# A fused graph network on one core: register loads of the one-hot loop gathered ahead of a wait, and the attribute split of the message loop spread over two steps

## What is computed

```python
x = x + L0(h, edges)          # mean of neighbours, two matrix products
x = x + L1(h, edges, noise)   # four transformer blocks with attention over edges
x = x + L2(h, edges, attr3)   # graph convolution; weight of an edge from 3 attributes
x = x + L3(h, edges, attr64)  # messages on edges
# L3:
edge_feat = concatenate([x[src], x[dst], edge_attr])   # 20000 x (512 + 512 + 64)
messages  = mish(mish(edge_feat @ W1 + b1) @ W2 + b2)
agg       = segment_sum(messages, dst)
# ... two more products on the nodes, a layernorm
```

## Time and profile before

| | us |
|---|---|
| median of 3 runs | 1679.72 |
| the runs | 1679.72, 1692.11, 1679.65 |
| profiled execution, its time | 1672.88 |
| profiled execution, its span | 1671.0 |
| busy in the span: PE / DVE / ACT / POOL | 1566.8 / 1190.2 / 1097.2 / 686.0 |

### The profile page before, as it was taken

How to read it: one execution, slowest core, us unless ns; L and a number is a source line. 1 busy time by engine, 2 the same in 40 slices (tenths; PEclk the granted TensorE clock), 3 DMA queues, 4 the chain that set the end, 5 groups by cost and what they waited for, 6 DMA issues and landing times. The chain is left out here.

```text
span 1671.0 us, 25082 instructions
## 1 busy us (share of the span) xinstructions
PE 1566.8 (94%) x8530; PEld 1218.3 (73%) x8530; DVE 1190.2 (71%) x1900; ACT 1097.2 (66%) x1531; POOL 686.0 (41%) x495
## 2 busy tenths in 40 slices
PE   5789699999999999999999999999999999999987
PEld 4765486878687868877854777777777777777774
DVE  8867546564655546565733588989989898998967
ACT  9841536554554455444530699999999999999962
POOL 3410120110012001200302788888888888888500
PEclk9999799999999999999999999999999999999989
DMA  3001140013002200211107767677777777777710
GB/s 104 0 19 65 39 133 25 1 51 113 26 20 67 85 21 32 62 52 63 53 1 228 156 139 150 145 144 148 138 152 144 148 145 142 151 135 155 162 38 31
DMA packets 107046, 153.94 MB, mean 92 GB/s; under 512 B 42042, under 2 KB 47034, under 8 KB 106466
## 3 DMA queue, kind: packets, MB, share of 16 engines
q0 software_dynamic: 72832, 87.84, 27.3%
q1 hardware_dynamic: 34146, 65.21, 12.0%
HBM read 141.02 MB, written 11.73 MB: 91 GB/s over the span
## 5 line engine op out<-in xcount | busy, mean ns | idle before, releaser
L1692 POOL DMA_INDIRECT edge_gathered<-dst_table,edge_index x158 | 257.3, 1629 | 57.4 <-issue 53.9
L222 PE MATMUL edge_z2p<-edge_w_hi,edge_h_hi 128*128 128x512 f32 x628 | 255.3, 407 | 6.8 <-issue 3.5
L1661 POOL DMA_INDIRECT edge_gathered<-src_table,edge_index x158 | 221.5, 1402 | 85.3 <-issue 33.6
L222 PE MATMUL edge_z2p<-edge_w_hi,edge_h_lo 128*128 128x512 f32 x628 | 248.5, 396 | 0.0
L222 PE MATMUL edge_z2p<-edge_w_lo,edge_h_hi 128*128 128x512 f32 x628 | 248.3, 395 | 0.0
L904 POOL TENSOR_TENSOR tr_cw<-w_c,tr_cw 32x1024 fp32r<-32x1024 f32 x8 | 19.0, 2373 | 367.5 <-ACT tr_cw L1118 367.5
L915 POOL TENSOR_TENSOR h<-h,tr_row_b 128x512 f32<-128x512 f32 x40 | 61.1, 1562 | 263.9 <-ACT C L1160 263.6
L222 PEld LDWEIGHTS edge_z2p<-edge_w_hi,edge_h_hi 128*128 128x128 f32 x628 | 117.9, 188 | 61.3 <-issue 36.3
L2020 DVE SCALAR_TENSOR_TENSOR edge_early<-edge_early,edge_z1p 128x1024 f32<-128x1024 f32 x79 | 96.5, 1221 | 59.8 <-ACT edge_early L1897 44.0
L222 PEld LDWEIGHTS edge_z2p<-edge_w_hi,edge_h_lo 128*128 128x128 f32 x628 | 118.0, 188 | 28.5
L222 PEld LDWEIGHTS edge_z2p<-edge_w_lo,edge_h_hi 128*128 128x128 f32 x628 | 118.1, 188 | 24.9
(11 more groups left out here) (356 smaller groups left out, 3985.8 us busy)
## 6 DMA issues: line engine op xcount, KB each, us to landing
w_c<-in_attr_T SPq DMA_DIRECT2D x78, 128.0 KB
agg<-edge_sum_rows POOLq DMA_DIRECT2D x36, 128.0 KB
w_a<-in_wv SPq DMA_DIRECT2D x4, 1024.0 KB, 5.3
w_b<-in_wq SPq DMA_DIRECT2D x4, 1024.0 KB, 5.4
w_a<-in_wk SPq DMA_DIRECT2D x4, 1024.0 KB, 7.7
w_b<-in_wo SPq DMA_DIRECT2D x4, 1024.0 KB, 7.0
w_a<-in_m SPq DMA_DIRECT2D x4, 1024.0 KB, 5.4
w_b<-in_m SPq DMA_DIRECT2D x4, 1024.0 KB, 5.3
```

The source lines that it names most:

```text
L222: mm = pe.matmul(out, a, b, start=(n == 0), stop=(n == last))
L1661: pool.indirect_dma_start(out=from_rows[a][:, j, :].bitcast(F32), out_offset=None, in_=k.src_table, in_offset=bass.IndirectOffsetOnAxis(ap ...
L1692: pool.indirect_dma_start(out=from_rows[ring][:, j, :].bitcast(F32), out_offset=None, in_=k.dst_table, in_offset=bass.IndirectOffsetOnAxis ...
```

## The change

In `front`, the loads of window starts: one for the two groups of a span in place of one for each group, in the prologue and in the loop. In the loop the start of the addition and the start of the two later compares are both loaded ahead of the wait on group_ready. In the two spans behind the loop the load also stands ahead of the wait.

In `edge_layer`, on DVE: the copy of the attribute split (L2040) moves from the end of the even step to the end of the odd step before it, for the group of the coming step; the subtraction stays. Its wait on z1_made asks for s(-1), in the odd step, where it was s(-2) in the even one. In step 0, which has no step before it, both stay together. The hand-written last steps follow the same conditions.

```diff
-                for a in range(RING):
-                    compare_to(a, a, start_of(a))
+                for a in range(0, RING, SHARE):
+                    start = start_of(a)
+                    for b in range(SHARE):
+                        compare_to(a + b, a + b, start)
...
-                def add_span(u, s, a):
-                    start = start_of(u)
+                def add_span(s, a, start):
                     dve.wait_ge(added, s + 2)
...
                         u = t * RING + a
+                        start, start_next = start_of(u), start_of(u + RING)
                         dve.wait_ge(group_ready, u + (SHARE + RING))
                         for b in range(SHARE):
-                            compare_to(u + (RING + b), a + b, start_of(u + (RING + b)))
-                        add_span(u, t * (RING // SHARE) + a // SHARE, a)
+                            compare_to(u + (RING + b), a + b, start_next)
+                        add_span(t * (RING // SHARE) + a // SHARE, a, start)
                         for b in range(SHARE):
                             compare_from(u + (RING + b), a + b)
                 for a in range(0, RING, SHARE):
+                    start = start_of(n * GROUPS + (GROUPS - RING + a))
                     dve.wait_ge(group_ready, n * GROUPS + (GROUPS + a + SHARE))
...
+                def attr_high(slot, group):
+                    dve.wait_ge(attr_loaded[slot], group // 2 * 32 + 32)
+                    dve.tensor_copy(attr_parts[slot][:, :], attr[slot][:, :]).then_inc(S["attr_high"], 1)
...
                     if a % 2 == 0 and on(0):
                         slot = a // 2
-                        dve.wait_ge(attr_loaded[slot], g(0) // 2 * 32 + 32)
-                        if on(4):
-                            dve.wait_ge(S["z1_made"], s(-2))
-                        dve.tensor_copy(attr_parts[slot][:, :], attr[slot][:, :]).then_inc(S["attr_high"], 1)
+                        if not on(1):
+                            attr_high(slot, g(0))
                         dve.wait_ge(S["attr_high"], g(-2))
                         dve.tensor_tensor(attr_parts[slot][high, :], ...).then_inc(S["attr_low"], 1)
+                    if a % 2 == 1 and on(-1):
+                        if on(3):
+                            dve.wait_ge(S["z1_made"], s(-1))
+                        attr_high((a + 1) % 4 // 2, g(-1))
```

More of the change, by code:

```diff
@@ L625, in _ @@
                 for a in range(0, RING, SHARE):
+                    start = start_of(n * GROUPS + (GROUPS - RING + a))
                     dve.wait_ge(group_ready, n * GROUPS + (GROUPS + a + SHARE))
-                    add_span(n * GROUPS + (GROUPS - RING + a), n * SPANS + (SPANS - RING // SHARE + a // SHARE), a)
+                    add_span(n * SPANS + (SPANS - RING // SHARE + a // SHARE), a, start)
                 dve.wait_ge(added, n * SPANS + (SPANS + 2))
```

## The result

The changed kernel takes 1664.38 us (median of 4 executions, 1662.46 to 1665.82) beside 1680.4 us of the kernel before in the same job (1679.65 to 1692.11); the ratio, which is one of means, is 0.989, with an interval of 0.984 to 0.993. By the medians that is 16.0 us less, where the forecast was 8.7. The profiled executions are closer to it: 1662.97 us (span 1661.3) against 1672.88 (1671.0), 9.9 less.

The account below looks back on a forecast made before the run. It took DVE to pace the one-hot loop and the message loop to run close to TensorE's own time; 2.0 + 6.4 + 0.3 = 8.7 us took the profiled 1672.88 to 1664.2, plus 6.8 gave 1671.0 us, range 1662 to 1682.

Parts of the forecast that it names:

- (a): One-hot loop, loads ahead of the wait and merged: 0 in steady periods, which stay 4.33 us under POOL's 2.04 us.
- (b): First and last period of the one-hot loop: 1.3 us and about 0.7 us sooner, sum 2.0 us, bounds 0.3 and 2.5.
- (c): Message loop, copy moved: double step 17.15 to 16.95 us, 6.4 us over 32, plus 0.3 at the loop's start.
- The step that failed: Timed median: the 6.8 us between profiled execution and median was carried over unchanged, from 1664.2 to 1671.0 us.
- The first (a shorter one-hot period): Rival, one-hot loop: first compare beats POOL's second multiply, up to 0.5 us per period, 7.5 more: 1663.5 us; chance 0.12.
- The second (the message loop keeps its rhythm): Rival, message loop: POOL holds DVE elsewhere, double step stays 17.15 us, only the one-hot loop's ends gain: 1677.7 us; chance 0.17.
- The third: Rival, message loop: L1977 held to the end of POOL's L1661, double step 0.28 to 0.50 us longer: 1687 to 1694; chance 0.13.

## Why the prediction was off, step by step

**(a) right.** The steady period stays 4.33 us, and the run without POOL's products shows that POOL is the cover and what it hides: 0.7 us a period, where the prediction had 0.5, since it counted only the addition's "issue" and not the load between the two compares, which costs 0.49 us in every second period once POOL is gone.

**(b) right in schedule.** First compare 22.15 (22.1 was forecast), last addition 2.03 us sooner (2.0). One reading in it was too short: the first period was put at 4.97 us "since two more loads stand between its instructions", but one load shows there, 0.50 us, and the second compare behind it takes 1.12 us beside POOL's product from 23.54 us. This is the pattern of the circle, and it stood in the very period that (b) priced. The tail alone put back makes the last two additions 3.73 us apart in place of 3.01, 0.72 for a term of 0.7; by medians it costs 1.0 to 1.6 us, within the spread. Of the 2.0 us, 0.65 were left in the profiled pair where the message loop's first product stands (876.91 against 877.56). Between the two points lie stretches that the change doesn't touch, and their length differs between profiles of one and the same kernel by as much (876.6 and 877.6 for before, 876.7 and 876.9 for the changed kernel), so the profiled pair can't tell how much of the 2.0 us is carried on. The prediction carried all of it without a row for these stretches.

**(c) right.** From the thirteenth transpose block, where both kernels run evenly, to the last double step the gain grows from 1.12 to 7.57 us: 6.45, forecast 6.4. The start adds 0.56 (forecast 0.3). Another 1.8 us come at the loop's very end, where TensorE's clock is at half for 10.2 us in place of 13.7; the sum had no such term, and it is luck: in the second profile of the changed kernel it is 13.7 us there, in one of the kernel before 10.2. 0.56 (at the first transposes) + 0.56 + 6.45 + 1.8 = 9.4 of the 9.7 us between the spans. So the profiled pair agrees with the sum (9.9 for 8.7) in part because 1.8 us of luck stand where 1.4 us of (b) are missing.

**The step that failed** is the last of the sum: "The median of the runs shown is 1679.72, 6.8 above the profiled one, and the same difference gives 1671.0." The profile of before was an execution without clock loss, and those 6.8 us were taken for something that stands outside of what the change touches. In the changed kernel the difference between median and profiled execution is 1.4 us. So that is the term that was wrong: 6.8 were kept and 1.4 were left. Of 87 executions of before that were timed beside the other kernels, the 42 with a mean clock of 0.985 or more have a median of 1674.0 us, the 45 below lie between 1673.6 and 1692.6, with a median of 1685.2; the median of all is 1678.0. So of the 6.8 us 1.1 lie between the profiled execution and the median of those that kept their clock, 4.0 go with loss of clock, and the three executions shown lay another 1.7 higher by the draw. The one-hot part alone came to 7.4 us by its ratio, with an interval of 2.7 to 11.9; 2.0 are schedule, and the other 5.4, an estimate by difference, go with the clock losses that it ends. The loop alone put back gives less on the median, 2.6 us with 1.3 of schedule in it, and more on the mean, 6.5. The prediction had the start of it: the earlier trace rows show a DVE wait with loads behind it; the pause of 2.0 us that this gave TensorE was not looked at, since the granted clock in that profile was 1.00 throughout the loop.

**The other term that was not seen** is that before's double step is 17.15 us only in part of its executions (four profiles of six). That makes (c) worth less on the median than in the profiled pair, by an estimate 4.3 us (four sixths of 6.4); the message part alone came to about 7 by its ratio, with an interval of 1 to 13, too wide to tell.

**The rivals.** The first (a shorter one-hot period) didn't come: 4.33. That its 1663.5 us is close to the 1664.38 measured is coincidence. The second (the message loop keeps its rhythm) fell with 13 profiles at 16.95. The third fell in the row at 1204.14: L1983 starts 0.14 us behind the start of POOL's L1663 (1204.00 to 1205.07) and takes 0.69 us, not held. The Trainium skill's rule of an exclusive lock for whole instructions (page "SBUF — State Buffer", section "SBUF: two separate sides") isn't borne out by this row, while the compares beside POOL's products (2.6 us with, 1.86 without; the one that starts at 34.70 ends just behind POOL's row) agree with it. The copy inside L1706 is longer than alone, but it isn't held to the end of that row: started at 1338.31, it ended at 1339.11, and L1706 at 1340.05.

## What to carry to other kernels

A register load behind a wait costs little while something covers it, but it makes every lateness of the other side longer by its own time and by what slips into the gap; place loads ahead of the wait even where a profile shows them free. When the executions of a kernel spread, one profile is one draw: look at the mean granted clock of each timed execution, and if the profiled one is among the shortest, take a second profile before the difference to the median is carried over unchanged. And where an engine's work collides with another's in a steady loop, ask whether the rhythm seen is the only one that the code allows.

## What was not expected of the hardware

- A TensorE pause of 2.0 us was followed by 3.4 us at 1.2 GHz in some executions and not in others of the same kernel. In five profiles without the fall the pause starts at 24.66 to 25.16 us, in three with it at 25.12, 25.24 and 25.70: the later ones fell, with one of each kind at nearly the same place, and whether the place is the cause was not tested.
- The lowered clock can keep itself up through another engine's waits: 3.67 and 6.69 us in turn in place of 4.33 and 4.33, three pairs in the profile that shows most.
- The same copy of 128x512 takes 0.42 to 0.47 us away from POOL's store L1706, 0.63 to 0.67 us near its end and 0.77 to 0.80 near its start, and a loop of 32 double steps runs at 16.95, at 17.15 or at 17.12 us in one and the same program, for many double steps on end.
- A gap of 0.49 us between two compares lets POOL's product in between them, and the second compare then takes 1.13 us in place of 0.42.
